# Two mixtures of experts rebuilt: relu gates spread over partitions, capacity rows gathered by a slot table, normed in the slots and scattered to the output

## What is computed

```python
sel_probs = sigmoid(x @ expert_sel.T)
sel_val = top4(sel_probs); sel_val = sel_val / clip(sel_val.sum(-1), 1e-9) * route_scale
scores_all = relu(einsum('btd,edh->bteh', x, keys))
values_all = einsum('bteh,ehv->btev', scores_all, values)
out = (take(values_all, top4_index) * sel_val).sum(axis=2)
x = layernorm(x + out)
```

```python
probs = softmax(tokens @ gate_w); expert_idx = argmax(probs)
mask1 = one_hot(expert_idx, 8); pos = cumsum(mask1, axis=0) - 1
sec_mask = mask1[:, :, None] * one_hot(pos, 320)
expert_input = einsum('tec,td->ecd', sec_mask, tokens)
h = relu(einsum('ecd,edf->ecf', expert_input, w1))          # f = 1024
expert_output = einsum('ecf,efd->ecd', h, w2)
out = einsum('tec,ecd->td', probs[:, :, None] * sec_mask, expert_output)
x = layernorm(x + out)
```

## Time and profile before

| | |
|---|---|
| runs | 3391.46 us median of 3 (3388.67 to 3393.8) |
| profiled execution | 3394.49 us, span 3392.7 us |
| TensorE busy | 3077.6 us (91%), mean granted clock 0.967 |
| VectorE, ScalarE, GpSimd busy | 49%, 36%, 9% |
| DMA | 85.14 MB, mean 25 GB/s |

### The profile page before, as it was taken

One profiled execution on the slowest core, in us unless ns is written; L12 is line 12 of the kernel. 1 busy time (PEld: TensorE's weight loads), 2 busy tenths in 40 slices (PEclk: granted clock), 3 DMA queues, 4 the chain that ended last, 5 costly groups with the idle time before them and its releaser, 6 DMA issues. The chain is left out here.

```text
span 3392.7 us, 56135 instructions
## 1 busy us (share of the span) xinstructions
PE 3077.6 (91%) x22954; PEld 1959.4 (58%) x22954; DVE 1659.0 (49%) x2939; ACT 1222.0 (36%) x2636; POOL 291.9 (9%) x511
## 2 busy tenths in 40 slices
PE   6999899999989998899999988989999899889695
PEld 3665566666658885556666655656655333346463
DVE  4665344444433234534444443225556999957112
ACT  1332244455431112235544441113323666623011
POOL 1111000000000000000000000000011000001102
PEclk9999999999999999799999999989999999989797
DMA  2001000000100002000000000000001000000432
GB/s 104 18 13 62 9 1 1 1 1 1 60 16 0 0 0 85 15 1 1 1 1 1 1 26 28 12 31 23 10 26 38 16 1 1 1 19 14 150 130 86
DMA packets 36410, 85.14 MB, mean 25 GB/s; under 512 B 3246, under 2 KB 30103, under 8 KB 32599
## 3 DMA queue, kind: packets, MB, share of 16 engines
q1 hardware_dynamic: 31831, 75.06, 6.3%
q0 software_dynamic: 1536, 4.20, 0.4%
q10 hardware_dynamic: 2816, 2.62, 0.2%
HBM read 53.90 MB, written 9.44 MB: 19 GB/s over the span
## 5 line engine op out<-in xcount | busy, mean ns | idle before, releaser
L2329 ACT ACTIVATE prob<-R,neg_max 128x333 f32<-128x333 f32 x512 | 268.8, 538 | 182.3 <-DVE neg_max L2399 182.3
L3420 DVE TENSOR_TENSOR_SCAN arena<-arena,u 128x512 f32<-128x512 f32 x256 | 289.5, 1201 | 0.1
L2399 DVE TENSOR_REDUCE neg_max<-R 128x2 f32<-128x666 f32 x256 | 205.6, 845 | 97.0 <-PE R L2209 97.0
L2220 PEld LDWEIGHTS T<-const,prob 128*128 128x128 f32 (+1 forms) x1536 | 183.3, 143 | 96.3 <-issue 66.2
L2405 DVE COPY prob_t<-T 128x384 f32<-128x384 f32 x256 | 141.6, 553 | 188.4 <-PE T L2220 183.2
L2220 PE MATMUL T<-const,prob 128*128 128x128 f32 (+1 forms) x1536 | 210.0, 273 | 19.7 <-DVE prob_t L2405 19.5
L2336 ACT ACTIVATE prob_t<-T 128x384 f32<-128x384 f32 x256 | 126.3, 493 | 213.2 <-PE T L2220 206.6
L3351 ACT ACTIVATE arena<-delta,neg_a 128x510 f32<-128x510 f32 x256 | 177.2, 717 | 46.7 <-DVE arena L3420 45.7
L2169 PE MATMUL O<-arena,keys_in 128*128 128x512 f32 (+1 forms) x384 | 183.8, 603 | 5.0 <-ACT arena L2310 2.4
L2164 PE MATMUL O<-keys_in,arena 128*128 128x333 f32 x512 | 170.3, 458 | 1.2 <-DVE arena L2380 1.2
L3257 PE MATMUL R<-arena,diag 64*64 64x512 f32 x1024 | 136.1, 622 | 24.6 <-DVE arena L3420 24.4
(11 more groups left out here) (463 smaller groups left out, 5488.1 us busy)
## 6 DMA issues: line engine op xcount, KB each, us to landing
w<-w_dram SPq DMA_DIRECT2D x16, 1024.0 KB, 7.1
arena<-pack_dram SPq DMA_DIRECT2D x2, 4100.0 KB, 15.0
q_pad<-q_pad SPq DMA_DIRECT2D x24, 224.0 KB, 2.7
arena<-pack_dram SPq DMA_DIRECT2D x4, 1284.0 KB, 6.0
arena<-pack_dram SPq DMA_DIRECT2D x1, 4896.0 KB, 15.3
arena<-k_nat SPq DMA_DIRECT2D x16, 224.0 KB, 2.7
arena<-arena SPq DMA_DIRECT2D x16, 224.0 KB, 2.8
arena<-pack_dram SPq DMA_DIRECT2D x1, 2707.0 KB, 14.8
```

What stands on the lines that cost most here:

```text
L2220: last = nc.tensor.transpose(S.T[0:n, i, kc * P:(kc + 1) * P], prob[:, g % 2, i, first:first + n], S.ident)
L2329: last = nc.scalar.activation(prob[:, g % 2, i, :], S.R[:, g % 2, i * BANK:i * BANK + XK], ACT.Exp, bias=neg_max[:, g % 2, i:i + 1], accum ...
L2399: nc.vector.tensor_reduce(neg_max[:, g % 2, :], S.R[:, g % 2, :].rearrange("p (i n) -> p i n", i=2)[:, :, 0:XK], AX.X, ALU.max, negate=Tru ...
L3420: nc.vector.tensor_tensor_scan(state[:, q % HELD, :], decay[:, q % DEEP, :], u[:, i % 2, :], 0.0, ALU.mult, ALU.add)\
```

## The change

**moe_relu.** `hidden` now has the weights `keys` as stationary operand and 256 tokens of `x_t` as moving one, so that its result has hidden units on partitions and needs no transpose. The gates must then lie along partitions too: VectorE splits them into three bf16 parts that add up to the float32 value (`gate_wide`), TensorE transposes them once (L2892), and per batch `spread` multiplies them with a 0/1 matrix `expand` (an addition to the weights, 8 x 128 columns), eight bf16 matmuls, which ScalarE copies to `gates`. VectorE's `clipped` joins relu and gate in one operation of 512 columns. `x_nat` is written directly, `xc`, `xres` and `yn` are not used, and the loops are written out with a batch's steps spread over three rounds.

**moe_capacity.** x goes to DRAM as it is (rows 1 to 2048; row 0 is a filler). A table `holds` says for each slot which row it holds: VectorE makes `at_place` (one-hot of the place in a tile of 128) and `at_tile` (expert and third, times the token's number), and 16 matmuls of 24 columns add them up; 16 more give the gate of each slot (`gate_of`). GpSimd gathers the 320 rows of an expert by three indirect DMAs, into four buffers. The third output tile is split in two halves of 128 columns, one on each half of the array's columns. Gate, residual and norm are done on the 320 rows of the expert (`normalised`), and GpSimd scatters them straight to the output, where slots without a token have a row number out of bounds. Before that, every row of the output is filled with the norm of x alone, which stays for tokens that no expert took.

```diff
@@ moe_relu, TensorE
-                    for at in (0, BANK):
-                        for c in range(C):
-                            last = nc.tensor.matmul(S.R[:, tt, at:at + BANK], x[:, c, tt * P:(tt + 1) * P], keys[:, c, at:at + BANK],
-                                                    start=(c == 0), stop=(c == C - 1))
...
-                        for i in range(4):
-                            last = nc.tensor.transpose(S.T[:, j, i * P:(i + 1) * P], hid[:, tt, (4 * j + i) * P:(4 * j + i + 1) * P], S.ident)
+            def hidden(b, g):
+                if b >= 1:
+                    pe.wait_ge(M.exp_done, G * (b - 1) + g + 1)
+                for h in range(2):
+                    for c in range(C):
+                        last = nc.tensor.matmul(hidden_bank(g)[:, h * T:(h + 1) * T], keys[:, c, (2 * g + h) * P:(2 * g + h + 1) * P],
+                                                S.x_t[:, c, b * T:(b + 1) * T], start=(c == 0), stop=(c == C - 1))
+                last.then_inc(M.s_full, 1)
+
+            def spread(b, half):
+                if b >= 1 or half:
+                    pe.wait_ge(M.kg_ready, 2 * b + half)
+                for h in range(4):
+                    c = 4 * half + h
+                    last = nc.tensor.matmul(S.T[:, h // 2, h % 2 * T:(h % 2 + 1) * T], expand[:, c * P:(c + 1) * P],
+                                            gate_t[:, b * T:(b + 1) * T], start=True, stop=True)
+                last.then_inc(M.st_full, 1)
...
@@ moe_relu, VectorE
+            def clipped(b, g):
+                dve.wait_ge(M.s_full, G * b + g + 1)
+                dve.wait_ge(M.kg_ready, 2 * b + g // 2 + 1)
+                nc.vector.scalar_tensor_tensor(hid[:, b % 2, 2 * g:2 * g + 2, :].rearrange("p c t -> p (c t)"), hidden_bank(g), 0.0,
+                                               gates[:, g // 2, g % 2, :], ALU.max, ALU.mult).then_inc(M.exp_done, 1)
...
@@ moe_capacity, TensorE
-                for t, n in ROWS:
+                for t in range(2):
                     for f in range(FC):
...
+                for f in range(FC):
+                    for h in range(2):
+                        last = nc.tensor.matmul(S.O[h * HB:(h + 1) * HB, 1, 0:P], hid[:, f, 2 * P:CAP], w2[:, s, f, h * P:(h + 1) * P],
+                                                start=(f == 0), stop=(f == FC - 1), skip_group_check=True)
...
@@ moe_capacity, VectorE
+            def normalised(e):
+                s = e % 2
+                dve.wait_ge(S.ln_rstd, e + 2)
+                for t, n in ROWS:
+                    last = nc.vector.tensor_scalar(ye[0:n, s, t, :], ye[0:n, s, t, :], slot_mv[0:n, s, t, 0:1], slot_rstd[0:n, s, t:t + 1],
+                                                   ALU.subtract, ALU.mult)
+                last.then_inc(S.ye_ready, 1)
...
+                    if j == 1 and e >= 1:
+                        normalised(e - 1)
...
@@ moe_capacity, GpSimd
-            for tt in range(NT):
-                nc.gpsimd.indirect_dma_start(S.xe_dram[:, :], bass.IndirectOffsetOnAxis(ap=to[:, tt:tt + 1], axis=0),
-                                             S.x_nat[:, tt, :], None).then_inc(S.scattered, 16)
...
+            for e in range(E3):
+                s = e % 2
+                pool.wait_ge(S.ln_stat, e + 2)
+                nc.gpsimd.tensor_tensor(slot_rstd[:, s, :], slot_mv[:, s, :, 1], neg_half[:, 0:3], ALU.pow).then_inc(S.ln_rstd, 1)
+                if e + 4 < E3:
+                    pool.wait_ge(S.xe_free[0], e + 1)
+                    gather(e + 4)
+                pool.wait_ge(S.ye_ready, e + 1)
+                for t, n in ROWS:
+                    nc.gpsimd.indirect_dma_start(out[:, :], bass.IndirectOffsetOnAxis(ap=dest[0:n, 3 * e + t:3 * e + t + 1], axis=0),
+                                                 ye[0:n, s, t, :], None, bounds_check=N - 1, oob_is_err=False).then_inc(S.sent[s], 16)
```

More of the change, by code:

```diff
@@ new lines, in transposed @@
+            def transposed(b):
+                act.wait_ge(M.yt_full, b + 1)
+                nc.scalar.activation(S.x_t[:, :, b * T:(b + 1) * T], S.O[:, 1, :].rearrange("p (c t) -> p c t", c=C), ACT.Copy)\
+                    .then_inc(M.xt_done, 1)
+            for i in range(B + 2):
+                if i < B:
+                    spread(i, 0)
+                    spread(i, 1)
+                if 0 <= i - 2 < B:
+                    transposed(i - 2)
+            settle(act, M.st_full, 2 * B)
@@ new lines, in result @@
+            def result(b):
+                dve.wait_ge(M.y_full, b + 1)
+                nc.vector.tensor_tensor(ysb[:, b % 2, :, :], S.O[:, 0, :].rearrange("p (t d) -> p t d", t=TT),
+                                        S.x_nat[:, b * TT:(b + 1) * TT, :], ALU.add).then_inc(M.y_read, 1)
+                dve.drain()
+                for tt in range(TT):
+                    nc.vector.bn_stats(bst[:, tt, :], ysb[:, b % 2, tt, :])
+                dve.drain()
+                for tt in range(TT):
+                    last = nc.vector.bn_aggr(mv[:, b % 2, tt, :], bst[:, tt, :])
+                last.then_inc(M.ln_stat, 1)
@@ new lines, in _ @@
+            nc.vector.tensor_copy(gate_wide[:, :, E:2 * E], gate_b[:, 1, :, :])
+            dve.drain().then_inc(M.setup, 1)
+            for i in range(B + 2):
+                if i < B:
+                    clipped(i, 0)
+                    clipped(i, 1)
+                if 0 <= i - 2 < B:
+                    normalised(i - 2)
+                if i < B:
+                    clipped(i, 2)
+                    clipped(i, 3)
+                if 0 <= i - 1 < B:
+                    result(i - 1)
@@ L2956, in int8_product @@
+            settle(pool, M.ln_stat, B)
 def int8_product(nc, S, k):
@@ new lines, in _ @@
+            dve.drain()
+            nc.vector.tensor_tensor(at_tile[:], one_hot[:].unsqueeze(3).to_broadcast([P, NT, E3, 3]),
+                                    parts[:].unsqueeze(2).to_broadcast([P, NT, E3, 3]), ALU.mult)
+            for half in range(2):
+                tiles, some = slice(half * NT // 2, (half + 1) * NT // 2), [P, NT // 2, P]
+                nc.vector.tensor_tensor(at_place[:, tiles, :], part(S.const, CONST, "count").unsqueeze(1).to_broadcast(some),
+                                        place[:, tiles].unsqueeze(2).to_broadcast(some), ALU.is_equal)
+                dve.drain().then_inc(S.h_ready, 1)
```

528 lines of the change are left out of this document (285 added, 243 removed).

## The result

The changed kernel takes **3331.87 us** (median of 4 runs, 3326.21 to 3335.16), the kernel before 3392.04 in the same series: ratio 0.9822, 95% interval 0.9805 to 0.9839. It is faster by 60 us, where 3321 (3308 to 3342) had been forecast against 3391.5. The profiled execution took 3335.16 us, with a span of 3333.2 and a mean granted clock of 0.973.

What follows compares the result with a forecast made beforehand. TensorE, busy 91%, was the busiest engine, every other under half. Gains 22.2 + 9.8 + 12 + 26.8 - 0.2 = 70.6 us took 3394.5 to 3323.9; the median, 3.0 us under, gave 3321, range 3308 to 3342.

Steps and rivals of the forecast that it cites:

- rival 2: Capacity start gains nothing: gathers queue behind store and weights, or GpSimd gathers slower; clock stays down; 3331 us, chance 0.12.
- rival 1: Experts' third tile is not halved, as one half's weight load waits for the other's matmul; 3333 us, chance 0.14.
- Relu stage: Relu mixture without transposes of the hidden layer: 154.6 us against 176.8, 22.2 us less, bounds 17 to 25.
- first output's delay: Relu stage's beginning: hidden(1) can start 26.5 us after the stage's start, where 25.3 passed before.
- clock allowance: Relu stage: 2.5 us of slow work allowed once, since TensorE waits about 4 us with little work.
- Capacity start: Last stage before its experts: first expert starts at 3173.9 instead of 3183.7, 9.8 us less, bounds 4 to 13.
- the table is in PSUM between 3158.2 and 3161.4; I take 3160: Capacity start: time when TensorE's 32 table instructions are done, priced at full to half clock.
- Experts: Capacity stage's eight experts: halved third tile takes 1.9 us instead of 3.5, 12 us less, bounds 0 to 14.
- rival 3: Both stages hide more: no relu clock loss, table at full clock, 1.7 us per third tile; 3312 us, chance 0.08.
- End: After the last expert's last matmul: 11.8 us instead of 38.6, 26.8 us less, bounds 23 to 28.
- lands in 2.8, and 0.4 closes: End: the third scatter lands 2.8 us after its start, and 0.4 us more closes the kernel.
- Rival 4: Experts: GpSimd's six indirect DMAs and a power become every expert's bound; slower than before; chance 0.02.

Runs made afterwards that it cites:

- relu_warm: Changed kernel plus four 128x512 keep-warm matmuls in the relu stage, two behind each of the first batch's two spreads; 3322.37 us, ratio 0.9792 to before.
- warm_table: Changed kernel plus four 128x512 matmuls of no use on TensorE right ahead of the slot table's matmuls; 3322.64 us, ratio 0.9782 to before.
- between: warm_table with four of the six keep-warm matmuls moved in one piece between the table's and the gates' narrow matmuls; 3314.02 us, ratio 0.9778 to before.
- best: Changed kernel plus warm_table's and relu_warm's wide matmuls, gate matmuls moved later, seven keep-warm behind the table, last expert's end split; 3311.66 us, ratio 0.9782 to before.
- third_whole: Changed kernel with the third tile's output not halved: 16 matmuls of 256 moving columns instead of 32 of 128; 3335.61 us, ratio 0.9841 to before.
- third_in_turn: Changed kernel with the third tile's 16 lower-half matmuls first, then the 16 upper-half ones, instead of alternating; 3333.15 us, ratio 0.9837 to before.
- gates_later: Changed kernel with the gates' matmuls moved behind the keep-warm matmuls and the first expert's transposes on TensorE; 3331.53 us, ratio 0.9814 to before.

## Why the prediction was right, and where its terms were off

- **Direction and mechanisms** held, and the time lay in the range, 10.9 us above the forecast. By its number alone, 3331.9 lies nearer to rival 2 (3331) and rival 1 (3333) than to the forecast; only the stages tell them apart. In the profiles that is 1.0 us in the relu stage, 4.7 at the capacity start, 2.0 at the end, less 1.5 in the experts, and 5.0 in stages that the change doesn't touch (11.2 together; the rest is how the medians stand to the profiles).
- **Relu stage**: 22.2 predicted, 21.2 found. Rounds 15.72 (15.6), hidden 7.2 (7.0), first output's delay and the clock allowance as priced: 6.25 less 3.72 is 2.5. With the two waits of 1.12 us for ScalarE filled by wide matmuls (relu_warm) this loss is gone; whether it came from the idle time or from having little wide work there, that run can't tell.
- **Capacity start**: 9.8 predicted, 5.1 found, the mis-sized term. The step that failed is "the table is in PSUM between 3158.2 and 3161.4; I take 3160", with gates and keep-warm behind it at 11.4 us together. 3160 is 18.4 us after the stage's start; the table was done 20.0 us after it. Both narrow stretches ran wholly at the lower clock (7.00 each, near the 6.7 of the bound), and the keep-warm matmuls took 8.0: 14.7 us. Both sums had counted part of this work at the upper clock. That is the one half of rival 2, "the clock stays down"; the other half is out, for the gathers, to which it gave the wait, were in time. warm_table, between and best won back 5.8, 8.8 and 11.1 us of the start by the clock and the order of this queue (5.8, 7.2 and 8.9 with what between and best lose in the experts).
- **Experts**: 12 predicted, 13.5 found, third tile 1.97 (1.9), by the mechanism of the earlier trace rows. The undivided tile had been taken too short: it costs 3.67 us (third_whole) and not 3.5, so 1.7 us are saved in each expert, the figure of rival 3. Rival 1 would have had 3.5; third_in_turn shows the overlap that it denies.
- **End**: 26.8 predicted, 24.8 found. The failed step is "lands in 2.8, and 0.4 closes": I had taken the landing from gathers, and the scatter to DRAM needs 5.1 us from its start to the end of the span, where 3.2 had been counted. What comes before it was priced rightly: the last scatter starts 8.8 us after the last matmul (8.7). The Trainium skill (DMA: Bandwidth & Descriptors, "Anatomy of one DMA — SWDGE (gpsimd) path") puts most of a DMA's fixed cost into the receipt of the last write, heaviest for DRAM; the order of the two rows agrees, but no run here takes those 5.1 us apart.
- **Rival 4** is out: in the experts' stretch GpSimd is busy 40.3 us of 156.9, and it waits for VectorE's statistics ahead of six powers (68.6 us in all, up to 12.2 at once) and 21.2 us ahead of another one for a DMA (out_dram<-arena; the view of waits).
- **The unchanged stages** were taken as fixed. They weren't: see the table. That they took 5.0 us more here, and not less, is chance.

## What to carry to other kernels

When an edit lengthens or shortens one stage by less than the unchanged stages vary, compare stage lengths inside the profiles: here 12.5 us in one stage (third_whole) left the median of four runs only 3.7 us higher. When something waits behind an engine's own queue, price each piece of that queue at the clock it will really have, and ask whether a piece of it may stand later. Work that reads nothing new (here keep-warm) is worth most where the engine would be idle anyway: four such matmuls in a wait of 5.8 us halved the time of what came next.

## What the runs showed of the hardware that was not expected

- Stretches of 24-column matmuls ran at granted clock 0.50 with TensorE busy throughout (13.7 us in the changed kernel). Begun at 1.00, 64 such instructions in a row lost the clock 5.3 us after their start in warm_table, and 32 lost it after 3.2 us in gates_later, while 32, then eight of 512 columns, then 32 did not in between.
- Two instructions with 64 weight columns on different column halves stream together: 32 of them in 1.97 us instead of 3.33 in turn. With the 0.27 us that one takes left out, they start 0.055 us apart instead of 0.099.
- The same unchanged stages took from 2046.3 to 2061.3 us in 14 profiles, in part by the clock: the stretch from 1300 to 1500 us had a granted clock of 0.88 in the kernel before and 0.94 in third_whole, the shortest. Not all of it is the clock: the two profiles of the changed kernel differ by 5.2 us there with a granted clock of 0.99 in both.
- From a scatter's start on GpSimd to the end of the program pass 5.1 to 5.2 us, where gathers had landed in 2.8.
